# Adding the shift before the convolution's product, and spreading the router's constants over the blocks of the MLP

## The reference, cut to what matters

```python
# end of the attention block's first half: x is the residual, xm the modulated normed input
y = causal_convolution(xm, K)                 # per channel, 64 taps: a 64x64 Toeplitz matrix
x = x + (y * film_scale + film_shift)         # film_scale, film_shift: [64, 64, 128]
# MLP with its own norm, then the outer norm and the router
h = gelu(layernorm(x, g_ffn, b_ffn) @ W1 + b1)        # 128 -> 512
x = x + h @ W2 + b2                                   # 512 -> 128
x = x_in + layernorm(x) * g_norm_out + b_norm_out
xn = layernorm(x)
logits = relu(xn @ rw1 + rb1) @ rw2 + rb2             # 128 -> 512 -> 8 experts, two largest taken
```

## Time and profile before

| | us |
|---|---|
| runs | 933.27, 924.9, 926.25 |
| median | 926.25 |
| profiled execution: its own time | 934.4 |
| its span, first to last instruction | 933.2 |
| convolution stage in it, about | 261.0 to 287.5 |
| MLP and router stage, about | 287.9 to 445.5 |
| of it the eight blocks, about | 287.9 to 413 |

### The profile page before, as it was taken

How to read it: one execution, slowest core, us unless ns; L and a number is a source line. 1 busy time by engine, 2 the same in 40 slices (tenths; PEclk the granted TensorE clock), 3 DMA queues, 4 the chain that set the end, 5 groups by cost and what they waited for, 6 DMA issues and landing times. The chain is left out here.

```text
span 933.2 us, 20728 instructions
## 1 busy us (share of the span) xinstructions
PE 726.7 (78%) x6170; PEld 510.4 (55%) x6170; DVE 674.3 (72%) x3212; ACT 475.0 (51%) x1318; POOL 565.1 (61%) x931
## 2 busy tenths in 40 slices
PE   0698999889993999972499438998888974799970
PEld 0354555555482656632276326765666652699970
DVE  6897999988433688668111066589989886699974
ACT  3566777555201465440133175577777761577740
POOL 7688877667536445200677667345877767277770
PEclk9888999778685999986599755799999885899995
DMA  6300115999014987600365330000000002698828
GB/s 143 57 26 7 42 45 67 86 93 113 17 46 199 268 261 250 215 11 1 41 115 132 100 123 1 2 2 14 25 26 26 25 28 83 214 274 265 260 70 270
DMA packets 98830, 94.41 MB, mean 101 GB/s; under 512 B 37512, under 2 KB 82303, under 8 KB 98143
## 3 DMA queue, kind: packets, MB, share of 16 engines
q1 hardware_dynamic: 91268, 79.34, 34.4%
q0 software_dynamic: 6592, 13.58, 6.0%
q10 hardware_dynamic: 858, 0.17, 0.1%
HBM read 47.76 MB, written 43.19 MB: 97 GB/s over the span
## 5 line engine op out<-in xcount | busy, mean ns | idle before, releaser
L2416 POOL DMA_INDIRECT expert_pairs<-e_ys,e_home x78 | 75.4, 967 | 38.6 <-issue 23.5
L1756 POOL TENSOR_SCALAR a_kb<-a_kr,a_m,a_bk 128x128 f32<-128x128 f32 x128 | 58.1, 454 | 46.2 <-ACT a_kr L1995 34.0
L1774 POOL DMA_INDIRECT expert_slots<-r_rows,r_slotu x64 | 63.3, 989 | 28.1 <-issue 13.6
L964 DVE MATCH_REPLACE8 work<-m,work 128x64 f32<-128x64 f32 x384 | 75.4, 204 | 0.0
L778 PE MATMUL side<-pen,ones 128*128 128x512 f32 x98 | 58.3, 719 | 13.4 <-ACT fold_done L305 7.0
L1498 POOL DMA_INDIRECT ex_rows<-rows,slot_source x32 | 30.7, 960 | 53.3 <-POOLq L1177 43.8
L951 DVE MAX8 m<-work 128x8 f32<-128x64 f32 x384 | 56.8, 206 | 0.0
L1829 PE MATMUL a_pss<-a_kb,a_qt 32*64 32x256 f32 x512 | 40.8, 447 | 15.7 <-ACT a_pp L1980 13.9
L2182 DVE TENSOR_REDUCE a_mx<-a_pss 128x8 f32<-128x512 f32 x64 | 43.8, 685 | 8.4 <-PE a_pss L1829 8.0
L2383 PE MATMUL e_ps<-e_XH,e_wh 128*128 128x256 f32 x156 | 48.3, 309 | 1.4 <-DVE e_XL L2428 1.4
L1550 ACT ACTIVATE ex_hs<-ex_psh,vec 128x512 f32<-128x512 f32 x32 | 22.0, 687 | 51.1 <-PE ex_psh L1531 50.5
(11 more groups left out here) (466 smaller groups left out, 2439.7 us busy)
## 6 DMA issues: line engine op xcount, KB each, us to landing
expert_slots<-rt_unfilled SPq DMA_DIRECT2D x151, 130.0 KB, 3.0
ahead<-folded_weights SPq DMA_DIRECT2D x20, 386.0 KB
e_wf<-folded_weights SPq DMA_DIRECT2D x19, 386.0 KB, 4.3
planes<-rt_zeros SPq DMA_DIRECT2D x4, 1024.0 KB
ew<-in_L_ffn_ew SPq DMA_DIRECT2D x16, 256.0 KB, 4.1
pair_y<-expert_pairs SPq DMA_DIRECT2D x16, 256.0 KB, 5.8
e_xr<-expert_slots SPq DMA_DIRECT2D x27, 130.0 KB, 3.2
folded_weights<-fold_done SPq DMA_DIRECT2D x8, 384.0 KB, 4.9
```

The source lines that it names most:

```text
L964: return own.did(dve.match_replace(wk_[x.j][:, h, :], m8[x.j][:, h, r, :], src[:, h, :], TAKEN))
L1756: m = pool.tensor_scalar(kb[a.j][:, :, h, :], k, m4[:, h:h + 1], bk4[:, h:h + 1], ALU.mult, ALU.add)
L1774: pool.indirect_dma_start(G.slots, bass.IndirectOffsetOnAxis(ap=slot[:, b, k, t:t + 1], axis=0), rb[b % NB][:, k, t, :], None).then_inc(se ...
L2416: pool.indirect_dma_start(G.pair, bass.IndirectOffsetOnAxis(ap=home[i % NY][:, k:k + 1], axis=0), ys[i % NY][:, k, :], None).then_inc(kept ...
```

## The change

In the convolution POOL adds the film shift to `XT` at once, for all eight groups and without waiting for anything; DVE then adds `ym` to `XT` itself, so that POOL no longer stands at the end of the chain, and `yn` goes. Behind the last group PE makes one product of constants (`ones` by a part of `pen`) whose result nobody reads. At the start of the MLP stage PE makes three more of such (`w1` by `rw1`). PE and ACT take the first product of block 0 ahead of the transposes of block 1. POOL's constants move behind its work for steps t = 1, 2 and 3; DVE writes the zeros, behind the statistics of block 1.

```diff
--- before.py
+++ after.py
@@ -1011,9 +1011,10 @@
     NG = D // CH
     with ExitStack() as ctx:
         psy = [C.ps(f"psy{j}", [P, CH, NT], ctx) for j in range(4)]
+        psw = C.ps("conv_warm", [P, 512], ctx)
+        held = G.pen[:, 0:512 // T, :].rearrange("p n t -> p (n t)")
         ym = [C.sb(f"ym{j}", [P, NT, CH], ctx=ctx) for j in range(2)]
-        yn = [C.sb(f"yn{j}", [P, NT, CH], ctx=ctx) for j in range(2)]
-        s = {n: C.sem("conv_" + n) for n in ("y", "y_film", "y_shift", "y_sum", "padded", "weights")}
+        s = {n: C.sem("conv_" + n) for n in ("y", "y_film", "shifted", "y_sum", "padded", "weights")}
         with nc.Block() as block:
 
             @block.sync
@@ -1035,9 +1036,7 @@
                 pool.memset(G.mlp["rw2"][:], 0.0).then_inc(s["padded"], 1)
                 for g in range(NG):
                     ch = slice(g * CH, g * CH + CH)
-                    pool.wait_ge(s["y_shift"], g + 1)
-                    pool.tensor_tensor(G.XT[:, :, ch], G.XT[:, :, ch], yn[g % 2][:], ALU.add).then_inc(s["y_sum"], 1)
-                    pool.wait_ge(s["y_sum"], g + 1)
+                    pool.tensor_tensor(G.XT[:, :, ch], G.XT[:, :, ch], G.FO[:, :, D + g * CH:D + g * CH + CH], ALU.add).then_inc(s["shifted"], 1)
 
             @block.tensor
             def _(pe):
@@ -1049,21 +1048,23 @@
                             mm = pe.matmul(psy[g % 4][rows, c, :], G.toe[rows, g * CH + c, :], G.XM[rows, :, g * CH + c],
                                            start=True, stop=True)
                     mm.then_inc(s["y"], 1)
+                for _ in range(1):
+                    pe.matmul(psw[:], G.ones[:], held, start=True, stop=True)
 
             @block.vector
             def _(dve):
                 for g in range(NG + 1):
                     if g < NG:
                         dve.wait_ge(s["y"], g + 1)
-                        after(dve, s["y_shift"], g - 1)
+                        after(dve, s["y_sum"], g - 1)
                         dve.tensor_tensor(ym[g % 2][:], psy[g % 4][:].rearrange("p c b -> p b c"),
                                           G.FO[:, :, g * CH:g * CH + CH], ALU.mult).then_inc(s["y_film"], 1)
                     if g > 0:
                         q = g - 1
                         dve.wait_ge(s["y_film"], q + 1)
-                        after(dve, s["y_sum"], q - 1)
-                        dve.tensor_tensor(yn[q % 2][:], ym[q % 2][:], G.FO[:, :, D + q * CH:D + q * CH + CH],
-                                          ALU.add).then_inc(s["y_shift"], 1)
+                        dve.wait_ge(s["shifted"], q + 1)
+                        kept = G.XT[:, :, q * CH:q * CH + CH]
+                        dve.tensor_tensor(kept, kept, ym[q % 2][:], ALU.add).then_inc(s["y_sum"], 1)
 
 
 def two_largest(dve, step, C, G, lg, w, iota):
@@ -1204,17 +1205,24 @@
             @block.gpsimd
             def _(pool):
                 step = Steps(pool, s["pool"])
-                step.then(pool.tensor_tensor(pick[:], G.ident[:, 0:32], G.ident[:, 32:64], ALU.add))
-                for c in range(2, NH):
-                    step.then(pool.tensor_tensor(pick[:], pick[:], G.ident[:, 32 * c:32 * c + 32], ALU.add))
-                pool.sem_inc(s["pick"], 1)
-                pool.iota(count_i[:], pattern=[[1, P]], base=0, channel_multiplier=0).then_inc(s["counts"], 1)
-                pool.iota(name_i[:], pattern=[[B * T, 2], [1, NT]], base=1, channel_multiplier=NT).then_inc(s["counts"], 1)
-                pool.iota(spare_i[:], pattern=[[P, NS2]], base=1 + 2 * B * T, channel_multiplier=1).then_inc(s["counts"], 1)
-                pool.memset(zeros[:], 0.0).then_inc(s["zeros"], 1)
-                step.did(pool.iota(unfilled_i[:], pattern=[[1, STILE // P]], base=SPARE, channel_multiplier=STILE // P))
-                step.then(pool.memset(unfilled[:], 0.0))
-                pool.tensor_copy(unfilled[:, :, D:D + 1].bitcast(U32).rearrange("p k a -> p (k a)"), unfilled_i[:]).then_inc(s["unfilled"], 1)
+
+                def pads():
+                    step.did(pool.iota(unfilled_i[:], pattern=[[1, STILE // P]], base=SPARE, channel_multiplier=STILE // P))
+                    step.then(pool.memset(unfilled[:], 0.0))
+                    pool.tensor_copy(unfilled[:, :, D:D + 1].bitcast(U32).rearrange("p k a -> p (k a)"), unfilled_i[:]).then_inc(s["unfilled"], 1)
+
+                def picks():
+                    step.then(pool.tensor_tensor(pick[:], G.ident[:, 0:32], G.ident[:, 32:64], ALU.add))
+                    for c in range(2, NH):
+                        step.then(pool.tensor_tensor(pick[:], pick[:], G.ident[:, 32 * c:32 * c + 32], ALU.add))
+                    pool.sem_inc(s["pick"], 1)
+
+                def counts():
+                    pool.iota(count_i[:], pattern=[[1, P]], base=0, channel_multiplier=0).then_inc(s["counts"], 1)
+                    pool.iota(name_i[:], pattern=[[B * T, 2], [1, NT]], base=1, channel_multiplier=NT).then_inc(s["counts"], 1)
+                    pool.iota(spare_i[:], pattern=[[P, NS2]], base=1 + 2 * B * T, channel_multiplier=1).then_inc(s["counts"], 1)
+
+                extra = {1: pads, 2: picks, 3: counts}
                 for t in range(-2, NBLK + 1):
                     for q, b in ((0, t + 2), (1, t - 1), (2, t - 1)):
                         if blk(b):
@@ -1225,23 +1233,32 @@
                         pool.wait_ge(s["xs"], t + 3)
                         pool.tensor_tensor(G.XT[:, rows, :], G.XT[:, rows, :], wide(b2[:].unsqueeze(1), [P, TB, D]), ALU.add)
                         pool.tensor_tensor(G.X[:, rows, :], G.X[:, rows, :], wide(bout[:].unsqueeze(1), [P, TB, D]), ALU.add).then_inc(s["biased"], 1)
+                    if t in extra:
+                        extra[t]()
 
             @block.tensor
             def _(pe):
-                for t in range(-1, NBLK + 3):
-                    if blk(t + 1):
-                        j = (t + 1) % 2
-                        pe.wait_ge(s["xs"], t + 2)
-                        after(pe, s["xf"], t + 1)
-                        after(pe, s["xf1"], t - 2)
-                        for k in range(TB):
-                            mm = pe.transpose(pst[:, k * P:(k + 1) * P], xs[j][:, k, :], G.ident[:])
-                        mm.then_inc(s["turned"], 1)
+                def turn(b):
+                    pe.wait_ge(s["xs"], b + 1)
+                    after(pe, s["xf"], b)
+                    after(pe, s["xf1"], b - 3)
+                    for k in range(TB):
+                        mm = pe.transpose(pst[:, k * P:(k + 1) * P], xs[b % 2][:, k, :], G.ident[:])
+                    mm.then_inc(s["turned"], 1)
+
+                for _ in range(3):
+                    pe.matmul(psy[1][:].rearrange("p k d -> p (k d)"), w1[:, 0:P], rw1[:], start=True, stop=True)
+                turn(0)
+                for t in range(NBLK + 3):
+                    if blk(t + 1) and t > 0:
+                        turn(t + 1)
                     if blk(t):
                         pe.wait_ge(s["xf"], t + 1)
                         for c in range(NH):
                             after(pe, r_sb[c], t - 2)
                             pe.matmul(psh[c][:], w1[:, c * P:(c + 1) * P], xf[t % 2][:], start=True, stop=True).then_inc(h_ps[c], 1)
+                    if t == 0:
+                        turn(1)
                     if blk(t - 3):
                         b = t - 3
                         after(pe, s["lg"], b)
@@ -1301,15 +1318,21 @@
             @block.scalar
             def _(act):
                 act.preload_act_table(ACT.Gelu)
-                for t in range(-1, NBLK + 3):
-                    if blk(t + 1):
-                        act.wait_ge(s["turned"], t + 2)
-                        act.activation(xf[(t + 1) % 2][:], pst[:], ACT.Identity, scale=G.vec[:, gv:gv + 1],
-                                       bias=G.vec[:, bv:bv + 1]).then_inc(s["xf"], 1)
+                def keep_turned(b):
+                    act.wait_ge(s["turned"], b + 1)
+                    act.activation(xf[b % 2][:], pst[:], ACT.Identity, scale=G.vec[:, gv:gv + 1],
+                                   bias=G.vec[:, bv:bv + 1]).then_inc(s["xf"], 1)
+
+                keep_turned(0)
+                for t in range(NBLK + 3):
+                    if blk(t + 1) and t > 0:
+                        keep_turned(t + 1)
                     if blk(t):
                         for c in range(NH):
                             act.wait_ge(h_ps[c], t + 1)
                             act.activation(hs[t % 2][:, c, :], psh[c][:], ACT.Gelu, bias=G.vec[:, b1 + c:b1 + c + 1]).then_inc(h_sb[c], 1)
+                    if t == 0:
+                        keep_turned(1)
                     if blk(t - 3):
                         b = t - 3
                         act.wait_ge(s["logits"], b + 1)
@@ -1348,6 +1371,8 @@
                         x = G.XT[:, b * TB:(b + 1) * TB, :]
                         after(dve, s["xs"], b)
```

(2 more changed lines are left out.)

## The result

| | before | changed |
|---|---|---|
| runs, us | 933.27, 924.9, 926.25, 927.98, 930.43, 925.04 | 917.78, 918.55, 918.67, 922.13, 914.89, 912.22 |
| median | 927.12 | 918.16 |
| ratio, 95% interval | | 0.9889, 0.9853 to 0.9925 |

The change makes the kernel faster by about 1.1%, with an interval on both sides of 1%. The forecast was 918.0. A later set of ten runs of the changed kernel has a median of 922.05 beside 928.63 of before, ratio 0.9937 (0.9895 to 0.9979); the two intervals overlap. By these ratios the gain is some 6 to 10 us, and the stages tell more of it than the totals do.

A forecast was written before the change was run, and what follows sets the result against it. PE bounds the MLP from block 2 on, a chain over POOL and DVE the start before it. 2.44 + 2.50 + 3.79 - 0.5 = 8.2 us off the median 926.25 gives 918.0 us, range 914.3 to 924.

The forecast's parts named there:

- End of the convolution: POOL's adds move to the front, so DVE's last add ends the convolution: 2.44 us off the path.
- DVE's adds against POOL's: In the convolution each DVE add may wait one POOL add, 1.26 us, hidden under PE's pace; costed at nothing.
- First inverse root: Start of the MLP stage: without constants in front POOL starts its first root 2.50 us earlier.
- First product ahead: Block 0's first product ahead of block 1's transposes: DVE's 4.27 us wait goes, POOL limits the gain to 3.79.
- rival 4: Clock in the runs of before rises later than in the profile: gain 8.2 to 11.9 us, about 916; chance 0.12.
- Rival 1: Clock stays low into the MLP's first product, block 0's second 2.0 us late: gain 6.2, 920; chance 0.13.
- What PE keeps: From block 0's xn on, PE, about 1.7 us early there, and DVE keep their distances; no cost counted.
- rival 3: Short pauses keep PE at half clock through the first blocks: 936 at worst, half of it 927 to 931; chance 0.06.
- if PE waits between blocks 2 and 7: MLP stage: a sign named beforehand that the prediction would be wrong; from block 2 PE should run without a gap.
- The 0.5 us for POOL's constants: Constants behind POOL's MLP steps may hold up DVE's last normalisations into `XT`: 0.5 us taken against the change.
- Rival 2: DVE's zeros hold up POOL in the first MLP blocks: up to 1.8 us, gain 6.4, 919.9; chance 0.07.
- rival 5: The MLP stage's end hangs on SP's DMAs, so the gain is lost: about 926; chance 0.04.

The follow-up runs named there:

- MLP only: The MLP stage as changed with the convolution as before the change; 921.13 us, ratio 0.9898 to before.
- sums behind: The changed kernel with five `ym` buffers and DVE's adds in the convolution only behind its fifth multiply; 918.51 us, ratio 0.9909 to before.
- paced kernel: The changed kernel, but POOL's add of group g in the convolution waits for DVE's multiply of group g - 2; 916.93 us, one run.
- conv only: The convolution as changed with the MLP stage as before the change; 922.1 us, ratio 0.9959 to before.
- constants in front: The changed kernel with POOL's constants and zeros in front of the first inverse root again; 923.98 us, ratio 0.9975 to before.

## Why the prediction was right

**End of the convolution**, 2.44 us: measured 2.57 at low clock, and 1.4 at full clock against the same old tail. The length of the product behind it was put at 1.7 us; it took 2.07 and ended at 276.41, DVE's tail at 276.34. So it is no longer covered, and costs 0.05 us: the tail is 2.25 in the two profiles without it.

**DVE's adds against POOL's.** The step "each DVE add may wait one POOL add, 1.26 us" failed: the first waited for all that were left, 6.08 us. PE wasn't stopped: its gap of 0.6 to 1.0 us in the convolution is there in the profiles with the old one too (0.99 in "MLP only"), so the 0.99 that I took for a wait in the expectation of "sums behind" is none; there 0.62 is left. The cost was nothing all the same where the clock fell, since DVE had caught up by the last group, and 1.2 us where it did not. The rule of the Trainium skill (SBUF — State Buffer, Who interferes with whom), that the two exclude each other for a whole instruction, agrees with the paced kernel (POOL's add 1.65 us instead of 1.25 where DVE's started first); that a queue of eight shuts the other out for as long as it lasts stands beyond it and is measured here.

**First inverse root**, 2.50: 3.88 - 1.38 = 2.50, and undone alone it costs 2.5 at DVE.

**First product ahead**, 3.79: DVE's add of block 0 was worked out at 15.3 us and came at 15.21; `mlp_nb` came at 295.91 - 276.71 = 19.20, before 25.54. Together with the root that is 6.34 at the xn of block 0, for 6.29 predicted. The agreement holds for the one profile that the term was read from. Its clock rose late, about 17 us into the stage; in "conv only", with the same old stage, it rose at about 15, and there the change gives 5.21. So 3.79 was too large by 1.1 for such a run, which the prediction didn't consider: its rival 4 looked only at a later rise. Rival 1 is out: the clock rose 4 us into the stage, and the first product, 2 us later, took 3.70 us.

**What PE keeps.** "From there DVE and PE keep the distances that they had" is the step that failed. I had worked out PE's pause ahead of xn 0 at 1.7 us and given it no price; it was 2.09, the clock fell, and of 6.34 us only 5.19 were left at xn 1. It is rival 3's mechanism at a small size: pauses at the start that cost clock. It is also one of the prediction's own signs of being wrong, "if PE waits between blocks 2 and 7": the pause lies between block 2's first and second product. Filling the pause gave the 1.1 us back. The fall came in six of the seven profiles that have this pause at 2.1 us, and in none of the other seven, where it is 0.39 to 1.32. In the one with the constants in front it did not come, and why is open.

**Rival 1's argument**, that the convolution keeps PE busy 20.87 of 22.40 us at a clock of 0.73, "so busy time alone doesn't hold it", passes over a gap of 0.90 us from 268.63, which ends 1.7 us ahead of the fall at 271.2. It is as open as the fall in the other convolutions.

**The 0.5 us for POOL's constants** was not paid: the normalisation into `XT` took 3.02 us with them behind it and 3.03 without. Rival 2 is out: POOL's bias adds beside DVE's zeros kept 1.27 us, and `mlp_xs` of block 1 started at 7.81. So is rival 5: the slot DMAs began 27.66 us into the stage (27.7 predicted), and the last of the row DMAs was issued by 390.96, 38 us ahead of the stage's end.

**The sum** was 8.2 for 7.6 between the two profiles, and the medians moved by 8.96 and, in the later set, by 6.6. It was in part luck. One price too many and one too few (0.5 and 1.1) lay near each other. And the clock rose late in the profile of before, not early as rival 4 had it: with the MLP stage of "conv only" in its place, what the change gives by xn 1 is 4.07, and with the tail's 1.4 to 2.6 some 5.5 to 6.6 us. That is nearer to the later set (ratio 0.9937, 5.8 us) than to the first one, whose median hit the forecast.

## What to carry to other kernels

Count a start-up stage as a chain over engines: here POOL's constants and an order that made PE wait for the second block cost 6.3 us in the profile that the arithmetic was read from, which gave that to 0.1, and 5.2 in another of the same code. Where the clock differs from run to run, read such a term from more than one profile. When an edit makes an engine early, ask what its new pause does to the clock, and price that. A run of instructions without a wait on POOL shuts DVE's two-operand adds out until the run is over: pace it, or put DVE's adds behind it (worth 1.2 us at most here).

## What the runs showed of the hardware

- In convolutions of nothing but small products (64x64 by 32 columns) the granted clock fell to 0.50 in eleven of thirteen profiles, 5.5 to 13.9 us in, each time 0.4 to 2.6 us behind a gap of 0.60 to 0.99 us on PE. Of the two where it stayed up, one has a gap of 0.62. One profile with seven products 128x256 between them has no gap and no fall.
- Behind the pause of 2.1 us ahead of xn 0 the clock fell in six profiles out of seven, and stayed low for about 3.4 us. In the seventh it stayed at 1.00 through that pause and one of 2.38 us before it. Pauses of 0.39 to 1.32 us at that place were followed by no fall in seven profiles.
- DVE writes 2048 float32 zeros per partition in 1.76 us, POOL in 1.81.
- The spread between runs, about 912 to 926 us for the changed kernel, comes for a good part from ahead of the change: the convolution started at 250.5 to 263.1 us in the fourteen profiles, in code that is the same in all. It goes with the granted clock over the first 250 us: 0.93 in the profile with the earliest start, 0.86 in the three with a start at 260.4, 261.1 and 263.1.
